# Attention row sums: reciprocals written to DRAM and read back spread over 64 partitions, in place of a widening multiply, two transposes and a copy

## The reference

```python
def attention(x, ctx, Wq, Wk, Wv, Wo, bo):
    q, k, v = (x @ Wq), (ctx @ Wk), (ctx @ Wv)      # split into 16 heads of 64
    sim = jnp.einsum('bihd,bjhd->bhij', q, k) * SCALE
    attn = jax.nn.softmax(sim, axis=-1)
    out = jnp.einsum('bhij,bjhd->bihd', attn, v)
    return out.reshape(b, n, HEADS * D_HEAD) @ Wo + bo
```

## Time and profile before

| | |
|---|---|
| median of 3 runs | 1081.24 us (1081.17 to 1081.41) |
| the profiled execution | 1081.92 us |
| its span in the trace | 1080.1 us |
| PE busy | 988.0 us (91%) |
| PEld busy | 927.1 us (86%) |
| DVE busy | 712.8 us (66%) |
| ACT busy | 625.8 us (58%) |
| POOL busy | 356.5 us (33%) |
| DMA moved | 34.60 MB, mean 32 GB/s |

### The profile page before, as it was taken

How to read it: one execution, slowest core, us unless ns; L and a number is a source line. 1 busy time by engine, 2 the same in 40 slices (tenths; PEclk the granted TensorE clock), 3 DMA queues, 4 the chain that set the end, 5 groups by cost and what they waited for, 6 DMA issues and landing times.

```text
span 1080.1 us, 21165 instructions
## 1 busy us (share of the span) xinstructions
PE 988.0 (91%) x7776; PEld 927.1 (86%) x7776; DVE 712.8 (66%) x1610; ACT 625.8 (58%) x1945; POOL 356.5 (33%) x474
## 2 busy tenths in 40 slices
PE   4688775499999999999999999999999998899998
PEld 4577654389999999999989889999999998899998
DVE  3466745496767666767667885776677667666664
ACT  2566443286657565657566765766676667534343
POOL 1101323133333333333342343554454454401010
PEclk9999888699999999999999998999999999999999
DMA  6221000100300000000000300300000001000100
GB/s 206 68 68 34 26 20 20 44 11 2 97 3 21 1 21 1 22 1 21 2 21 2 103 18 9 104 25 2 25 26 10 17 21 58 12 30 21 41 30 20
DMA packets 30444, 34.60 MB, mean 32 GB/s; under 512 B 4360, under 2 KB 23816, under 8 KB 30344
## 3 DMA queue, kind: packets, MB, share of 16 engines
q1 hardware_dynamic: 30344, 33.26, 10.2%
HBM read 24.86 MB, written 8.39 MB: 31 GB/s over the span
## 4 chain that ended last, share of the span: by engine, by line
PE 77%; DVE 10%; ACT 7%; issue 2%; POOL 1%; DMA 1%; SPq 1%; DVEq 0%; POOLq 0%
PE bank L1324 14%; PE bank L1325 14%; PE bank L1326 14%; PE bank L1549 8%; PE bank L1532 5%; PE bank L1336 5%; PE bank L1590 3%; PE bank L1591 3%; PE bank L1592 3%; PE bank L1564 3%; ACT p L737 2%; PE bank L1440 1%; PE bank L1506 1%; DVE bn L903 1%; DVE hT_lo L1089 1%
## 5 line engine op out<-in xcount | busy, mean ns | idle before, releaser
L737 ACT ACTIVATE p<-bank,negmax 128x256 f32<-128x256 f32 (+1 forms) x512 | 208.2, 428 | 18.4 <-DVE negmax L1106 15.5
L554 POOL TENSOR_TENSOR oT_hi<-oT,ones 128x256 fp32r<-128x256 f32 x128 | 93.7, 732 | 370.7 <-DVE oT L1129 370.7
L747 ACT CAST pT_hi<-bank 128x512 fp32r<-128x512 f32 (+1 forms) x256 | 110.8, 486 | 166.1 <-PE bank L1549 165.9
L1324 PE MATMUL bank<-hT_hi,w_hi 128*128 128x256 f32 x640 | 190.8, 298 | 6.3 <-DVE hT_lo L1089 2.5
L1326 PE MATMUL bank<-hT_hi,w_lo 128*128 128x256 f32 x640 | 181.6, 284 | 0.0
L1325 PE MATMUL bank<-hT_lo,w_hi 128*128 128x256 f32 x640 | 181.4, 283 | 0.0
L1324 PEld LDWEIGHTS bank<-hT_hi,w_hi 128*128 128x128 f32 x640 | 122.7, 192 | 9.9 <-DVE hT_lo L1089 4.8
L1121 DVE TENSOR_TENSOR pT_lo<-bank,pT_hi 128x512 fp32r<-128x512 f32 (+1 forms) x256 | 129.9, 550 | 0.5
L1102 DVE TENSOR_REDUCE negmax<-bank 128x2 f32<-128x512 f32 x128 | 82.2, 684 | 66.8 <-PE bank L1532 66.8
L1325 PEld LDWEIGHTS bank<-hT_lo,w_hi 128*128 128x128 f32 x640 | 123.1, 192 | 0.0
L1326 PEld LDWEIGHTS bank<-hT_hi,w_lo 128*128 128x128 f32 x640 | 122.8, 192 | 0.0
(11 more groups left out here) (202 smaller groups left out, 2737.8 us busy)
## 6 DMA issues: line engine op xcount, KB each, us to landing
w_stage<-in_weights SPq DMA_DIRECT2D x47, 256.0 KB, 4.5
x_in<-x_dram SPq DMA_DIRECT2D x24, 256.0 KB, 2.9
x_dram<-x_out SPq DMA_DIRECT2D x16, 256.0 KB, 3.2
l_x<-in_x SPq DMA_DIRECT2D x4, 512.0 KB, 5.0
x_dram<-l_out SPq DMA_DIRECT2D x4, 512.0 KB, 2.8
out_dram<-x_out SPq DMA_DIRECT2D x8, 256.0 KB, 3.1
w_stage<-in_weights SPq DMA_DIRECT2D x9, 128.0 KB, 5.1
l_ctx<-in_ctx SPq DMA_DIRECT2D x4, 180.0 KB, 4.4
```

The source lines that it names most:

```text
L554: nc.gpsimd.tensor_tensor(oh[:, G % PAIRS, :], of[:, :], ones[:, :], ALU.mult).then_inc(y["o_hi"], 1)
L737: last = nc.scalar.activation(p[:, G % 2, e, t * cols:(t + 1) * cols], scores_at(G, e, t), ACT.Exp, bias=negmax[:, G % 2, t, e:e + 1], acc ...
L747: nc.scalar.copy(pTh[0:r, G % 2, e, 0:n], bank[4 + e][0:r, 0:n]).then_inc(y["pT_hi"], 1)
L1324: nc.tensor.matmul(dst, lh, rh, start=(i == 0), stop=False)
```

## The change

The widening, the two transposes and the copy go. `inverse_sums` writes the reciprocals sorted by head, SP sends them to a DRAM buffer of 2 x 2 x 256 numbers (`send_sums`), and reads each head's row of 256 back to 64 partitions (`spread_sums`, two DMAs). `rsumT` gets a second buffer, and its order along the row is (q, t), so `normalise_o` reads it with a stride. SP's loop goes by steps now: in step G it sends the sums of G and spreads those of G - 1, then issues what falls due of loads, stores, context and weights, at set values of i.

```diff
-                rsw = sb("rsum_wide", [128, 2, NT, 2 * DH], where=att)
-                rT = sb("rsumT", [128, S], where=att)
+                rT = sb("rsumT", [128, 2, S], where=att)
...
+        sums_dram = nc.dram_tensor("rsums_dram", (2, 2, S), F32, kind="Internal").ap()
...
+            def send_sums(G):
+
+                sp.wait_ge(y["rsum"], G + 1)
+                if G >= 2:
+                    sp.wait_ge(y["rT"], 32 * (G - 1))
+                sp.dma_start(sums_dram[G % 2, :, :].rearrange("e (q t) -> q e t", t=NT),
+                             rs[:, G % 2, :].rearrange("q (e t) -> q e t", e=2)).then_inc(y[f"rsum_row{G % 2}"], 16)
+
+            def spread_sums(G):
+
+                sp.wait_ge(y[f"rsum_row{G % 2}"], 16 * (G // 2 + 1))
+                if G >= 2:
+                    sp.wait_ge(y["o_norm"], G - 1)
+                for e in range(2):
+                    sp.dma_start(rT[e * DH:(e + 1) * DH, G % 2, :], sums_dram[G % 2, e:e + 1, :].partition_broadcast(DH)
+                                 ).then_inc(y["rT"], 16)
+
             load(0)
             load_context(B)
             load(1)
-            load(2)
-            for b in range(3 * B):
-                if b + 3 < 3 * B:
-                    load(b + 3)
-                store(b)
-                if B < b + 3 < 2 * B:
-                    load_context(b + 3)
-                if b == 0:
-                    load_weights(sp, 12, 16)
-                if b == 6:
-                    load_weights(sp, 16, 20)
-                if b == 8:
-                    load_weights(sp, 20, 24)
-                if b == 14:
-                    load_weights(sp, 24, 26)
+            for G in range(STEPS):
+                b, i = divmod(G, PAIRS)
+                send_sums(G)
+                if G >= 1:
+                    spread_sums(G - 1)
+                if i == 3 and b >= 1:
+                    store(b - 1)
+                if i == 4:
+                    load(b + 2)
+                if i == 5 and B < b + 2 < 2 * B:
+                    load_context(b + 2)
+                if b == 1 and i < 4:
+                    load_weights(sp, 12 + i, 13 + i)
+                if b == B - 1 and i >= 2 and i < 6:
+                    load_weights(sp, 14 + i, 15 + i)
+                if b == B + 1 and i < 4:
+                    load_weights(sp, 20 + i, 21 + i)
+                if b == 2 * B - 1 and i in (6, 7):
+                    load_weights(sp, 18 + i, 19 + i)
+            sp.wait_ge(y["rT"], 32 * (STEPS - 1))
+            spread_sums(STEPS - 1)
+            store(2 * B - 1)
+            for b in range(2 * B, 3 * B):
+                if b + 2 < 3 * B:
+                    load(b + 2)
+                store(b)
...
-            def widen_sums(G):
-                pool.wait_ge(y["rsum"], G + 1)
-                nc.gpsimd.tensor_tensor(rsw[:, G % 2, :, :].rearrange("p t (e d) -> p (t e) d", e=2),
-                                        rs[:, G % 2, :].unsqueeze(2).broadcast_to([128, NT * 2, DH]),
-                                        ones[:, :].rearrange("p (n d) -> p n d", d=DH), ALU.mult
-                                        ).then_inc(y["rsum_wide"], 1)
...
-            def copy_rT(G):
-                act.wait_ge(y["o"], G + 1)
-                nc.scalar.copy(rT[:, :], bank[6][:, S:2 * S]).then_inc(y["rT_copied"], 1)
...
             def inverse_sums(G):
                 dve.wait_ge(y["exp"], 2 * G + 2)
-                nc.vector.reciprocal(rs[:, G % 2, :], expsum[:, G % 2, :, :].rearrange("p t e -> p (t e)")
+                if G >= 2:
+                    dve.wait_ge(y[f"rsum_row{G % 2}"], 16 * (G // 2))
+                nc.vector.reciprocal(rs[:, G % 2, :].rearrange("p (e t) -> p e t", e=2), expsum[:, G % 2, :, :].rearrange("p t e -> p e t")
                                      ).then_inc(y["rsum"], 1)
...
             def normalise_o(G):
-                dve.wait_ge(y["rT_copied"], G + 1)
+                dve.wait_ge(y["rT"], 32 * (G + 1))
+                dve.wait_ge(y["o"], G + 1)
                 if G >= 1:
                     dve.wait_ge(y["o_lo"], G)
-                nc.vector.tensor_tensor(of[:, :], bank[6][:, 0:S], rT[:, :], ALU.mult).then_inc(y["o_norm"], 1)
+                nc.vector.tensor_tensor(of[:, :].rearrange("p (t q) -> p t q", t=NT),
+                                        bank[6][:, 0:S].rearrange("p (t q) -> p t q", t=NT),
+                                        rT[:, G % 2, :].rearrange("p (q t) -> p t q", t=NT), ALU.mult).then_inc(y["o_norm"], 1)
...
-                pe.wait_ge(y["rsum_wide"], G + 1)
                 if G == 0:
                     pe.wait_ge(zeros_ready, 1)
                 if G >= 1:
                     pe.wait_ge(y["o_norm"], G)
-                for t in range(NT):
-                    nc.tensor.transpose(bank[6][:, S + t * 128:S + (t + 1) * 128], rsw[:, G % 2, t, :], ident[:, :])
```

More of the change, by code:

```diff
@@ L270, in build @@
             "cT_hi", "cT_lo", "qk", "qk_hi", "qk_lo", "v", "v_hi", "v_lo", "scores", "negmax", "exp", "rsum",
-            "rsum_wide", "pT", "pT_hi", "pT_lo", "o", "rT_copied", "o_norm", "o_hi", "o_lo", "wo", "up", "gelu", "glu",
+            "rsum_row0", "rsum_row1", "rT", "pT", "pT_hi", "pT_lo", "o", "o_norm", "o_hi", "o_lo", "wo", "up", "gelu", "glu",
             "f_hi", "f_lo", "down")}
         NI = B // L0B
+        sums_dram = nc.dram_tensor("rsums_dram", (2, 2, S), F32, kind="Internal").ap()
         def wcols(name, kt, lo_col, n):
@@ L560, in step @@
                 b, i = divmod(G, PAIRS)
-                widen_sums(G)
                 if i == 0:
@@ L802, in step_self @@
                     weights_hi(act, 10 + i)
-                if G >= 1:
-                    copy_rT(G - 1)
             def step_cross(G):
@@ L845, in feed_forward @@
                     if j == 1 and it == 0:
-                        copy_rT(STEPS - 1)
                         weights_hi(act, 25)
```

## The result

The changed kernel takes 1105.24 us (median of 4 runs, 1104.36 to 1105.89), against 1081.20 us before on the same chip: ratio 1.0224 (95% interval 1.0208 to 1.0240), so slower by 24 us, where 25 us less was forecast. The profiled execution took 1105.38 us, its span is 1103.6 us.

A forecast was written before the change was run, and what follows sets the result against it. PE was taken to bound both stages, but for one gap a sequence in cross attention. Transposes save 26.4 us, less 1.4 for weights and stage turns: 25 us off 1081.24 gives 1056.2 us; range 1051 to 1084.

The forecast's parts named there:

- What bounds the kernel: Self attention bound by PE alone, 51.70 of 51.70 us; cross attention by PE but for one 1.10 us gap a sequence.
- The transposes at 0.22 us: Two PE transposes a step go: 14.1 us saved in self attention, 12.3 in cross attention, sum 26.4 us.
- POOL and ACT at nothing: POOL's 79.9 us and ACT's 49.3 us of removed work lie off the path and count as nothing.
- L = 3.6 us: Time from the reciprocals of step G + 1 to `rsumT` of step G having landed; ends 3.4 and 4.0 us.
- At half of it they cost nothing. I take nothing: The write's 8-byte runs ahead of the spreads: at most 0.4 us more, counted as nothing, kept for the range.
- The threshold at L = 3.9: Cross attention: PE stays the bound up to here; above, each 0.1 us costs 6.4 us; gain gone at 4.3.
- D(i): Delay carried through a cross sequence's eight gaps, D(i-1) + L - gap(i), never below 0; longest 1.47 us, all hidden.
- The clock: PE's clock was read as full speed (1.00) in the sequences of both self and cross attention.
- Rival 2: Slower than before: 8-byte runs ahead of the spreads put L above 4.3; 1093 us at 4.5, 1119 at 4.9; chance 0.18.
- What moves: Stores, loads, context and weights issued behind the sums: 1.4 us lost for weights and turns between stages.
- The sign by which the text said it would be wrong: Cross attention: DVE waiting for `rsumT` in nearly every step, with periods of one length, would mean the loop rules.

The follow-up runs named there:

- half-way kernel: Changed kernel with the way through DRAM in steps 0 to 63 only, the old widening, transposes and copy from step 64 on; 1068.20 us, 0.9872.
- nothing sent: Changed kernel without its three DMAs a step and the waits for them, outputs multiplied by a constant 0.01; 1062.1 us, 0.9825.
- the kernels with L = 3.30 and 3.76: Changed kernel, spreads reading fixed numbers: without the write, 1064.10 us; with the write replaced by 16 runs of 128 bytes to DRAM, 1072.50 us.

## Why the prediction was wrong

- **What bounds the kernel**, PE in both stages: right for the kernel before. With the DMAs gone cross attention ran at 35.3 us a sequence, where the clock was full.
- **The transposes at 0.22 us**: right. 14.1 us were forecast in self attention; 12.2 came with the half-way kernel (409.5 - 397.3), 12.6 with nothing sent. The interval that was to be 0.24 us is 0.24: in the changed kernel the last projection matmul starts at 440.58, the second of the product at 440.82.

```profile
440.58 0.28 PE L1343 MATMUL bank<-hT_hi,w_lo 128*128 128x256 f32 x1
440.70 0.28 PE L1341 MATMUL bank<-pT_hi,v_hi 128*128 128x256 f32 x1
440.82 0.28 PE L1342 MATMUL bank<-pT_lo,v_hi 128*128 128x256 f32 x1
```

  In cross attention 12.3 us were forecast; nothing sent gave 299.0 - 293.2 = 5.8, since half the clock was granted for some 29 us of the stage, against some 18 before (2 x 0.03 x 299.0); half of that difference is 5 to 6 us of the missing 6.5.
- **POOL and ACT at nothing**: right. With both relieved and nothing sent, the time is PE's saving and no more.
- **L = 3.6 us**: the term that failed. Its parts were 0.04 for SP's wake, 0.51 for the write, 0.49 for the first spread and 0.04 for DVE; measured are 0.03, 0.46, 0.50 and 0.02. The landing of the second spread was taken as 2.5 us, with ends of 2.3 and 2.9. The best that it does is 2.65 us in the median behind an early write; behind a late one it is 3.92. In the cross stage its mean is 3.42 us, so this term was short by 0.9 us, which is all that L was short (3.6 against 4.49), and the upper end of 4.0, 4.4 with the runs, was below the mean. The prediction sets 2.0 us of fixed cost from the Trainium skill (DMA: Bandwidth & Descriptors, Anatomy of one DMA) beside its 2.5; that section is about DMAs issued by GpSimd, and these are issued by SP, where no second spread of the changed kernel landed in under 2.58 us.
- **"At half of it they cost nothing. I take nothing"**: here the choice went wrong. The runs' cost was bounded by the mean packet's time, 58 ns. A packet's own time was 9 ns, less than that, and the cost was none of it: it is in the time to landing, which no row of before had for such runs. The bound was made in the wrong unit. A write like none in the trace should have had an upper end from the slowest landing shown, 4.8 us of line 442, and that end alone passes the threshold of 3.9.
- **The threshold at L = 3.9**: right as an average, wrong as the place where the loss begins. It rests on averages, D(i) that never builds up and long gaps that absorb the rest. Two of its readings are off as well: of the eight gaps three are shorter than L = 3.6, not four, and the delays add up to 3.45 us a sequence, not 3.2. At a mean L of 3.76, with three landings in four within 0.2 us of each other, the cross stage lost 9.7 us. With all L together above it, 64 x (4.49 + 0.51 - 4.41) = 38 us would be lost; measured are 36.8. That agreement may be luck: a part of the 36.8 is clock, and the formula gives nothing for the 9.7. Even with L as forecast the sum would not have come out: the kernels with L = 3.30 and 3.76 took 1064 and 1072.5 us, not 1056.
- **The clock**: the forecast took full speed in the cross stage. The account above puts 12.6 of the 36.8 us on a PE that is busy longer with the same work. The stretches at half speed, 41 us of the stage against 27 with nothing sent, account for about 7 of them (half of the 14). The rest isn't taken apart; a matmul is shown 0.28 us long where the next can start after 0.12, so short pauses can count as busy.
- **Rival 2** named the place, the 8-byte runs of the write ahead of the spreads, and the point of decision, L = 4.3. Its mechanism, packets that take long, was not what happened. Its 1093 us at L = 4.5 lie 12 us under the measured 1105. The range stopped at 1084 us, short of it.
- **What moves** (-1.4): the first part is 1.4 us longer and the last 2.9; with nothing sent they are 217.2 and 154.5 us. So some 4 us of the loss lie at the ends; they aren't taken apart.
- The sign by which the text said it would be wrong was DVE waiting for `rsumT` in nearly every cross step, with periods of one length. The waits came: in 48 of the 64 cross steps, where three of eight (i = 0, 3 and 6) were forecast. The one length didn't: the cross steps took 4.1 to 7.6 us, with quartiles of 4.76, 5.31 and 5.55, since L itself varies. PE too waited more than before, for `normalise_o` 27.6 us in the cross stage against 14.6.

## What to carry to other kernels

A round trip through DRAM pays for PE's time where the step has room for its late landings and not only for its best ones: here the steps of 6.25 us hid all but 4.4 us of waits in 64 steps and those of 4.41 us did not, and using it in the one stage alone beat both kernels. Price a DMA by the longest time to landing that the trace shows for anything like it, and treat short runs to DRAM that are in flight beside a load that someone waits for, ahead of it or behind it, as a cost of their own. Where PE is the bound, waits put into it cost more than their length, since half clock can follow.

## What the runs showed of the hardware

- Behind a write of 2 KB to DRAM in 256 runs of 8 bytes about half of the loads landed late: in 3.92 us in the median where the write itself was late, against 2.65 us. Behind the same bytes in 16 runs of 128 bytes they did not (quartiles 2.61 to 2.77 us), nor behind 256 runs into SBUF (median 2.6 us); in both the loads read a buffer that the write left alone. Issued 0.68 us ahead of such a write instead, with no unfinished write before them, 56 of 128 loads took 3.3 us or more.
- The write itself landed in 3.2 us in the median in 256 runs to DRAM, in 1.9 us in 256 runs to SBUF, and in 1.3 us in 16 runs to DRAM.
- A DMA whose slowest dimension is 2 ran at 48 GB/s, at a busy share of 0.13 of the 16 DMA engines; a 256 KB store of the same kernel reached 363 GB/s.
- PE at half clock for 71 us of a stage of 323.5 us whose PE was idle for only 24.3 us in all.
